# Two LSTM recurrences on one core: a third one-hot buffer, and another order of VectorE's work in the cells of the second recurrence

## The reference, cut to what matters

```python
# B = 2048 samples; all sums in fp32, gate order i, f, g, o
def lstm_last(x, Wx, Wh, b):                      # x: [B, T, E]
    def step(carry, xt):
        h, c = carry
        i, f, gg, o = jnp.split(xt @ Wx + h @ Wh + b, 4, axis=-1)
        c = sigmoid(f) * c + sigmoid(i) * tanh(gg)
        return (sigmoid(o) * tanh(c), c), None
m_from, m_to = (lstm_last(base_emb[s], seq_Wx, seq_Wh, seq_b) for s in (from_seq, to_seq))   # T=64, H=64, 85 rows
x   = concat([nwf_num_emb[set][nums], nwf_freq_emb[set][freqs]])       # 11 features, 6 sets of 1000 rows, 4 + 4 wide
nwf = vmap(lstm_last)(x, nwf_Wx, nwf_Wh, nwf_b)                        # T=32, H=8
feats = concat([goby_emb[..], bool_emb[..], bool_emb[..], m_from, m_to, count_emb[..], count_emb[..], nwf])
return relu(feats @ reduce_W + reduce_b)
```

## Time and profile before

| what | value |
| --- | --- |
| median of 3 runs | 1712.02 us (1709.75 to 1712.13) |
| the profiled execution's own time | 1714.94 us |
| its span, first to last instruction | 1713.1 us |
| PE busy | 1610.2 us (94%) |
| DVE busy | 1509.0 us (88%) |
| ACT busy | 1314.0 us (77%) |
| POOL busy | 955.3 us (56%) |
| DMA queues' share of 16 engines, the one that SP issues to | 81.8% |
| one round in the steady stretch, a window from one L cell's add_c to the next | 51.35 us |
| granted TensorE clock in that window | 1.00 |

### The profile page before, as it was taken

One profiled execution on the slowest core, in us unless ns is written; L12 is line 12 of the kernel. 1 busy time (PEld: TensorE's weight loads), 2 busy tenths in 40 slices (PEclk: granted clock), 3 DMA queues, 4 the chain that ended last, 5 costly groups with the idle time before them and its releaser, 6 DMA issues.

```text
span 1713.1 us, 57020 instructions
## 1 busy us (share of the span) xinstructions
PE 1610.2 (94%) x23780; PEld 619.1 (36%) x23780; DVE 1509.0 (88%) x1573; ACT 1314.0 (77%) x2011; POOL 955.3 (56%) x473
## 2 busy tenths in 40 slices
PE   3799999999999999999999999999999999999997
PEld 0233333333333333333333333333333333333334
DVE  6788988989988989988989988988988988988984
ACT  4577777877777877777877778877778877778874
POOL 1445666776666776666754444554444554444553
PEclk8899999999999999999999999999999999999999
DMA  8678789898889898889788789899889888788870
GB/s 285 223 253 261 248 263 276 264 276 271 256 268 284 250 284 260 270 264 284 251 287 262 260 263 277 260 275 267 273 265 280 256 277 274 256 267 273 248 241 24
DMA packets 165793, 444.19 MB, mean 259 GB/s; under 512 B 45728, under 2 KB 103584, under 8 KB 132640
## 3 DMA queue, kind: packets, MB, share of 16 engines
q1 hardware_dynamic: 162112, 439.63, 81.8%
q0 software_dynamic: 2560, 0.15, 0.6%
q10 hardware_dynamic: 864, 0.75, 0.1%
HBM read 423.42 MB, written 6.82 MB: 251 GB/s over the span
## 4 chain that ended last, share of the span: by engine, by line
PE 53%; DVE 17%; ACT 15%; issue 9%; POOL 2%; DVEq 0%; POOLq 0%; ACTq 0%
PE e_ps L479 16%; PE ab L619 11%; PE f_ps L619 9%; PE ab L511 7%; DVE kept L493 7%; ACT gate L673 5%; DVE f_ps L705 5%; DVE seq_c L710 4%; ACT f_ps L671 3%; PE ab L425 3%; ACT tanh_c L664 3%; PE ab L560 2%; POOL ig L697 2%; ACT f_ps L673 2%; PE ab L570 2%
## 5 line engine op out<-in xcount | busy, mean ns | idle before, releaser
L697 POOL TENSOR_TENSOR ig<-gate 128x1024 f32<-128x1024 f32 x192 | 411.9, 2145 | 696.3 <-ACT seq_x L432 293.7
L479 PE MATMUL e_ps<-hot,tab 128*32 128x512 bf16 x8448 | 527.5, 384 | 61.6 <-DVE kept L493 56.8
L493 DVE SCALAR_TENSOR_TENSOR kept<-high,cst,e_ps 128x1024 f32<-128x1024 uint8 x352 | 449.1, 1276 | 49.6 <-PE e_ps L479 43.8
L619 PE MATMUL ab<-seq_h,seq_wh 64*64 64x512 f32 x3024 | 401.2, 590 | 0.0
L479 PEld LDWEIGHTS e_ps<-hot,tab 128*32 128x32 bf16 x8448 | 214.0, 97 | 486.8 <-issue 342.7
L469 DVE TENSOR_SCALAR hot<-low,cst 128x4096 bf16<-128x4096 bf16 x256 | 320.6, 1281 | 13.2 <-PE e_ps L479 13.2
L731 POOL TENSOR_TENSOR seq_h<-gate,tanh_c 128x1024 f32<-128x1024 f32 x128 | 308.9, 2414 | 31.8 <-ACT tanh_c L664 31.6
L673 ACT ACTIVATE gate<-ab,nwf_bias 128x512 f32<-128x512 f32 (+2 forms) x384 | 188.4, 553 | 166.2 <-PE ab L570 103.0
L671 ACT ACTIVATE gate<-ab 128x1024 f32<-128x1024 f32 x256 | 262.5, 1026 | 17.6 <-PE ab L619 8.8
L664 ACT ACTIVATE tanh_c<-seq_c 64x512 f32<-64x512 f32 (+1 forms) x384 | 241.9, 630 | 29.8 <-POOL nwf_h L731 22.1
L664 ACT ACTIVATE gate<-ab 64x512 f32<-64x512 f32 (+1 forms) x384 | 228.5, 595 | 9.4
(11 more groups left out here) (99 smaller groups left out, 1809.1 us busy)
## 6 DMA issues: line engine op xcount, KB each, us to landing
low<-low_digits SPq DMA_DIRECT2D x256, 1024.0 KB
low<-low_bytes SPq DMA_DIRECT2D x96, 512.0 KB
tok<-seq_tokens SPq DMA_DIRECT2D x128, 384.0 KB
high<-high_digits SPq DMA_DIRECT2D x1408, 32.0 KB
nwf_hq<-nwf_h SPq DMA_DIRECT2D x62, 128.0 KB
raw<-in_indices SPq DMA_DIRECT2D x32, 176.0 KB
low_digits<-low_of SPq DMA_DIRECT2D x32, 88.0 KB, 3.2
nwf_hq<-nwf_h SPq DMA_DIRECT2D x62, 32.0 KB, 3.0
```

The costliest lines, as they stand in the source:

```text
L479: last = nc.tensor.matmul(e_ps[32 * g:32 * g + 32, i, :], tab[:, part, 2 * m + ty, :], hot[:, p % HOT_RING, g, i, :], start=(part == 0), s ...
L493: nc.vector.scalar_tensor_tensor(out=kept[:, p % KEPT_RING, :, :], in0=wanted, scalar=cst[:, C_HIGH:C_HIGH + 1], in1=e_ps[:, :, :], op0=AL ...
L619: last = nc.tensor.matmul(flat(bank)[to:to + 64, cols], lhs(rows, half, block), rhs(rows, block, a, b), start=start, stop=stop)
L697: nc.gpsimd.tensor_tensor(ig[:, cols], gates[0][:, n % 2, cols], gates[1][:, n % 2, cols], ALU.mult).then_inc(ig_ready, 1)
```

## The change

The `hot` ring has three buffers instead of two; the distance of the compares stays two pairs (`COMPARED = 2`), so a compare no longer needs the look-up of the pair that is being masked. In S and in L the first compare of the cell stands ahead of the mask of p0. The digits of rounds 3 and later are made in S, behind the mask of p0, three cells earlier than before, where they stood in L between the two compares. POOL's `input_product` in a cell that makes digits waits for them too.

```diff
-ROUND_AT = {(0, 3)[_r - 1] if _r < 3 else NUMBER["nwf", _r - 2, 0]: _r for _r in range(FIRST_ROUNDS, NWF_T)}
+ROUND_AT = {(0, 3)[_r - 1] if _r < 3 else NUMBER["nwf", _r - 3, 1]: _r for _r in range(FIRST_ROUNDS, NWF_T)}
...
-LOW_RING, HIGH_RING, HOT_RING, KEPT_RING = 4, 5, 2, 5
+LOW_RING, HIGH_RING, HOT_RING, KEPT_RING = 4, 5, 3, 5
+
+COMPARED = 2
...
-                for p in range(HOT_RING):
+                for p in range(COMPARED):
                     compare_pair(dve, p)
...
-                    compared = [p + HOT_RING for p in pairs if p + HOT_RING < ALL_PAIRS]
+                    compared = [p + COMPARED for p in pairs if p + COMPARED < ALL_PAIRS]
+                    if CELLS[n][0] == "nwf":
+
+                        for p in compared[:1]:
+                            compare_pair(dve, p)
+                        compared = compared[1:]
                     for p in pairs[:1]:
                         keep_wanted(dve, p)
...
+                    if n in ROUND_AT and CELLS[n][0] == "nwf":
+                        make_digits(dve, ROUND_AT[n])
                     for p in compared[:2]:
                         compare_pair(dve, p)
-                        if p == compared[0] and n in ROUND_AT and CELLS[n][0] == "nwf":
-
-                            make_digits(dve, ROUND_AT[n])
...
                     for p in PAIRS_AT[n][:2][-1:]:
-                        pool.wait_ge(hot_ready, min(p + HOT_RING + 1, ALL_PAIRS))
+                        pool.wait_ge(hot_ready, min(p + COMPARED + 1, ALL_PAIRS))
+                    if n in ROUND_AT:
+                        pool.wait_ge(digits_made, ROUND_AT[n] + 1)
                     input_product(pool, n)
```

## The result

The changed kernel takes 1748.2 us (1746.56 to 1748.85, 4 runs) against 1710.88 us (1709.21 to 1712.13, 4 runs): ratio 1.0217, 95% interval 1.020 to 1.0235. It is slower, by 37 us; the forecast was +28.4 us, to 1741, with a range of 1714 to 1750.

What follows compares the result with a forecast made beforehand. The bound was taken to be a loop through the engines, where only earlier masks help. 29 x (0.22 + 0.75) = 28.1, plus 1.3 for rounds 30 and 31, about -1 for round 0: +28.4, to 1741 us, range 1714 to 1750.

Steps and rivals of the forecast that it cites:

- The exclusion: A compare meeting POOL's new_h stands until it ends: 1.57 us in L, about 1.35 in S, about 1.15 in B0.
- L: +0.22 forecast: L cell: the compare ahead delays PE's look-up of p1 and ACT's f, so add_c comes 0.22 us later.
- the 0.98: PE's idle time in us before A0's look-up of p0, waiting for a mask; it was to vanish.
- S: +0.75 forecast: S cell: POOL's ig waits for the digits and add_c for ig, costing 0.75 us a round, at most 0.78.
- one of the signs of being wrong: add_c in B1 standing at the same distance from S's as before would mean S's loss was made up.
- The gathers: POOL's gathers in rounds 2 to 15 stand ahead of no one who is late, so they cost nothing.
- The last rounds: Rounds 30 and 31, without digits: L loses 0.22 + 0.43, S nothing; together 1.3 us.
- -1 for the ring: Round 0: the three buffers take away a wait of 1.16 before a compare once, about -1 us.
- rival 1: The compares run beside new_h, so L gains 0.54 us a round: 1696 us; chance 0.13.
- against 2: Only one of the cells L and S pays, +0.2 to +0.5 a round: 1718 to 1727 us; chance 0.17.
- against 3: The two effects cancel, L gaining what S loses: 1709 to 1715 us; chance 0.08.
- DMA: Digit stores and raw load move to B0's place in SP's queue; costed at nothing.

Runs made afterwards that it cites:

- after_yield_l: The changed kernel with POOL made to wait for L's first compare before the new_h that ran beside it; 1725.6 us, ratio to before 1.0082.
- ahead_digits_in_l: The changed kernel with the digits back in L, behind the first mask and ahead of the second compare; 1720.2 us, ratio to before 1.0064.
- ring_alone: The kernel before with three one-hot buffers and nothing moved; 1711.6 us, ratio to before 1.0007.
- digits_in_s_only: The changed kernel with no compare ahead of a mask, digits in S behind the mask, then the compare; 1721.5 us, ratio to before 1.0066.
- after_no_digits_wait: The changed kernel without POOL's wait for the digits; 1806.0 us, ratio to before 1.0554.

## Why the prediction was right, point by point

- **The exclusion: right, in each size.** The first compare was to take 1.57 in L and 1.35 in S, and the seq compare in B0 about 1.15; they took 1.65, 1.45 and 1.10. L464 ends about 0.55 behind new_h. The prediction's page of the Trainium skill ("SBUF — State Buffer", "Who interferes with whom") says that whoever starts first holds the shared ports for the whole instruction. The traces agree: new_h, begun first, keeps its 2.39 (905.74) while L464 is held. after_yield_l moves the held time from the first compare to the second by nothing but the order. A row of before that the prediction did not use said the same of L462, of which it says that no row shows it beside a new_h: the new_h at 53.21, begun in the middle of the L462 at 52.96, took 5.11, with an L465 and an L469 behind.
- **L: +0.22 forecast.** The cell is 11.73 from add_c to add_c (877.89 to 889.62) against 11.48, +0.25; ahead_digits_in_l shows it by itself (+0.21 in the round). The steps hold as well: PE waits 1.05 (1.12 forecast), the 0.98 is gone, ACT's f is late and limits scale_c. That L makes no digits any more had no worth: ahead_digits_in_l makes them there, and its L is as long (1010.80 to 1022.54, 11.74).
- **S: +0.75 forecast.** From L's add_c to S's it is 24.68 (889.62 to 914.30) against 23.83, +0.85; add_c waits for ig, which waits for the last digit instruction. From S to B0 it is 7.77 against 7.79. About 0.15 comes back between B0 and L, which is the difference between 0.25 + 0.85 and the 0.92 of the round. Here a step failed in a small way: I held that nothing would return any of it. And one of the signs of being wrong was worded the wrong way round. By my own sum add_c of B1 keeps its distance from S's; had the loss of S been made up, it would be 0.85 shorter. It is 15.84 (914.30 to 930.14) against 16.01 (891.73 to 907.74), so most of the loss stayed.
- **The gathers: the step that failed.** "The gathers of the rounds 2 to 15 stand behind new_h and ahead of no one who is late; nothing." They cost 0.85 us a round, 11 us in 13 rounds (53.13 instead of 52.28), and 13.8 us by the medians with and without them. The number still fell into the range, by 2 us: room was left there for other things, and that it held this one too is luck. B0's ig stands behind the gather of S, and after the change it is late. I had moved new_h of A1 by 1.8 us in my sum and had not moved the gather that follows it on the same queue. The Trainium skill, same page, section "SBUF: two separate sides", describes it: a DMA issued by POOL needs the shared ports to write its descriptors and starves while DVE works in a two-port mode. The trace agrees: 0.98 us alone, 3.64 beside a seq compare and two compares. The trace of before had a sign of it as well, 2.33 for the gather behind new_h of A1; the prediction says that only the first cells show POOL and the compares at once.
- **The last rounds.** I added 1.3 us for the rounds 30 and 31. From L of round 29 to the end it is 127.19 (1747.1 - 1619.91) against 127.66 (1713.1 - 1585.44): -0.5. Round 30 was 0.7 longer, as forecast for L. Round 31 gave it back, and this is the ring's: before, the second compares of B0 and B1 there waited 0.92 and 0.55 for a look-up, and round 31 is 49.8 in ring_alone too, where before has 50.5. My sum had given the ring a gain in round 0 only. The rest lies behind L of round 31.
- **The sum.** Start -0.5, 13 rounds x 1.72 = 22.4, 14 rounds x 0.90 = 12.6, end -0.5: 34.0, the difference of the spans. Forecast +28.4: too little by the gathers, about 10.7 us (13 x 0.82), and too much by about 5 in the rest. Of these 5, 1.8 are the end and 1.9 the 27 rounds of 0.90 instead of 0.97. The other 1.4 are the start: I had -1 for the ring and +1.9 for the rounds 1 and 2, and these two rounds together are as long as before (109.89 against 109.95); why they lose nothing is open. So the two errors partly cancel. By the medians the change is 37.3, the profiled execution of before having taken 1714.94, 4 above its median.
- **The rivals.** The compare does not run beside new_h (rival 1); both cells pay (against 2); nothing cancels (against 3). What rival 1 hoped to win in L (0.54) is there to be had in another way: with no digits and no compare ahead, L gains 0.61 in digits_in_s_only.
- **DMA.** The move of the stores in SP's queue costs nothing that is seen: no instruction of DVE waits for a DMA after the first 100 us of the trace after.

## What to carry to other kernels

Where two engines exclude each other, an idle place on one is only free if the other is not busy there: lay the other's timeline beside it before an instruction is moved in, and do the same for every instruction that the move delays, DMAs issued by POOL included. The mark of such a loss is busy time that grows with the same number of instructions. And moved work need not be moved whole: 2 us did not fit in the quiet cell, 1 us did, and 1 us was all that the full cell had to lose.

## What I had not expected of the hardware

- A gather on POOL (DMA_INDIRECT) took 0.98 us when DVE left it alone and up to 3.69 when it met DVE's fast compares back to back. In the kernel before it got in between two of them, in a pause of 0.29 (2.33 in all).
- A blocked instruction's length follows when POOL's ends: L464 (0.75), L338 (0.33) and L360 (0.25) all took what was left of POOL's instruction and about 0.1 to 0.55 more, so a small instruction can suffer most in proportion (0.25 to 2.32).
- The mask, scale_c and add_c, each with at least one operand in PSUM, showed the same length beside POOL's instructions as alone in all these runs (1.27, 1.22, 1.22).
- In after_no_digits_wait the granted clock fell to 0.50 for one look-up in every second round, behind 2.18 us without a matmul; in the rounds between, the same idle time of 2.17 left it at 1.00.
